# GpSimd takes over the epsilon add of the attention denominators

## The chip, the core and the metric

The kernel runs on one core of a Trainium2 chip. Its engines work at their own pace and wait for each other by semaphores: TensorE (PE: matmuls, with its weight loads as PEld), VectorE (DVE), ScalarE (ACT), GpSimd (POOL) and SyncE (SP), which here issues the DMAs. The metric is the device time of one execution in microseconds (us), the median of several runs.

## The reference, cut to what matters

A batch of 8 sequences of 512 positions and 128 features passes through 8 layers of linear attention with a feed-forward part, and beside them through a small routed expert network that gates the result. The part that the change touches is the normaliser of the attention:

```python
q = _phi((h @ wq + bq_).reshape(b, s, H, DH))      # H = 16 heads, DH = 8, _phi = elu + 1
k = _phi((h @ wk + bk_).reshape(b, s, H, DH))
kv = jnp.einsum('bshd,bshm->bhdm', k, v)
z = 1.0 / (jnp.einsum('bshd,bhd->bsh', q, k.sum(axis=1)) + 1e-06)
att = jnp.einsum('bshd,bhdm,bsh->bshm', q, kv, z).reshape(b, s, d)
h = _ln(h + att @ wo + bo_, g1_, be1_)
y = gelu(h @ w1 + c1_) @ w2 + c2_
h = _ln(h + y, g2_, be2_)
```

## The kernel before

A unit `u` is one sequence in one layer: `u = 8 * l + b` for layer `l` and sequence `b`, 64 units in all. Every engine runs an order written out by hand, a software pipeline of periods. In period `p`, PE does the key, value and output products of unit `p` (`pe_kz`, `pe_kv_ksum`, `pe_kvo`, `pe_att`), the feed-forward products of unit `p - 2` (`pe_up`, `pe_down`) and the key and query projections of unit `p + 1` (`pe_kq`).

DVE in period `p` makes the denominators of unit `p`: `dve_q_ks` multiplies q by the key sums, `dve_den` sums over each head into `den` (128x64), `dve_blocks` masks the key-value product, `dve_rden` adds the epsilon into `den_e` and takes the reciprocal `rden`, and `dve_q_n` scales q by it. Between the last two stand the small shift operations (`m_r` and `shift`) and the four normalisations of `dve_norm1` for unit `p - 1`, whose result PE transposes, ACT copies (`z1_hi`) and DVE splits (`dve_z1_lo`). `dve_k_floor` for unit `p + 1` follows `dve_kvo`; it counts the semaphore `tk`. In the trace, `z1_tm` and `z_tm` are both shown as `z_tm`, `z1_lo` as `z_lo`, and `w2_use` as `w_use`.

GpSimd computes the residuals in the form that the adds of DVE need. In its period `p` it makes `res_att` of unit `p` (line 1008 multiplies, line 1011 adds, both 128x512), which `dve_h1` reads in DVE's period `p + 1`, and then `res_ffn` of unit `p - 2` (lines 1019 and 1022), which `dve_h2` reads in DVE's period `p`. `pool_res_ffn` waits for `tk` to reach `u + 3`, which is the end of `dve_k_floor` of unit `p`, in DVE's period `p - 1`. So GpSimd is ahead of DVE: it makes `res_att` of unit `p` at the start of DVE's period `p - 1`, once `h1` of unit `p - 2` is done, and `res_ffn` of unit `p - 2` late in that same period.

Beside the residuals, GpSimd copies the weights of a new layer into place. With `b == 0` it copies `w_v` after `res_att` and `w_o` after `res_ffn` (`pool_wo`); with `b == 2` it renews `g_ffn` and `ffn_row` ahead of `res_ffn` and copies `w2_use` behind it (`pool_w2`, 128x512). PE waits for these copies in the period of the same number: `w_o` in front of `pe_kvo` with `b == 0`, and `w2_use` in front of the first two tiles of `pe_down` with `b == 2`. This holds for layers 1 to 7; layer 0 has its weights early.

Of the kernel before, what the change touches and what calls it, by code (L numbers as in the profile page):

```python
# [8 lines left out]
DEN_EPS = 1e-6  # L9


def build(nc, x, Wq, bq, Wk, bk, Wv, bv, Wo, bo, g1, be1, g2, be2, W1, c1, W2, c2, gf, bef,
# [4 lines left out]
    ALU = mybir.AluOpType  # L17
# [18 lines left out]
    with ExitStack() as ctx:  # L36
        def sb(name, shape, dt=F32):
            return ctx.enter_context(nc.sbuf_tensor(name, shape, dt))
# [4 lines left out]
        def sem(name):  # L43
            return ctx.enter_context(nc.semaphore(name))
# [65 lines left out]
        den = sb("den", [P, HT])  # L110
        den_e = sb("den_e", [P, HT])
# [42 lines left out]
        s = {n: sem(n) for n in names}  # L154
# [117 lines left out]
        def pool_qk(pool, l):  # L272
            pool.wait_ge(s["fold_a"], l)
            pool.wait_ge(s["kqproj"], l * SEQS)
            pool.sem_inc(s["pool_waited"], 1)
            nc.gpsimd.tensor_copy(w_kq_hi[:, :], fold_att[:, 0:2 * D]).then_inc(s["qk_ready"], 1)
            pool.wait_ge(s["qk_ready"], l * 2 + 1)
            nc.gpsimd.tensor_tensor(w_kq_lo[:, :], fold_att[:, 0:2 * D], w_kq_hi[:, :].bitcast(F32),
                                    ALU.subtract).then_inc(s["qk_ready"], 1)

        def pool_wv(pool, l):
            pool.wait_ge(s["kv_ps_s"], l * SEQS)
            pool.sem_inc(s["pool_waited"], 1)
            nc.gpsimd.tensor_copy(w_v[:, :], fold_att[:, 2 * D:3 * D]).then_inc(s["wv_ready"], 1)

        def pool_wo(pool, l):
            pool.wait_ge(s["kvo_ps_s"], l * SEQS)
            pool.sem_inc(s["pool_waited"], 1)
            nc.gpsimd.tensor_copy(w_o[:, :], raw_wo[:, :]).then_inc(s["wo_ready"], 1)

        def pool_att_rows(pool, l):

            pool.wait_ge(s["t2m"], l * SEQS)
            pool.sem_inc(s["pool_waited"], 1)
            nc.gpsimd.tensor_copy(g_att[:, :], raw_g[:, 0, :]).then_inc(s["gatt_ready"], 1)
            nc.gpsimd.tensor_tensor(att_row[:, :], row_sum[:, 0, :], raw_g[:, 0, :], ALU.subtract).then_inc(s["gatt_ready"], 1)
# [331 lines left out]
        def is_unit(u):  # L628
            return not isinstance(u, int) or 0 <= u < UNITS
# [4 lines left out]
        def after_first(u):  # L634
            return not isinstance(u, int) or u > 0

        def is_layer(l):
            return not isinstance(l, int) or l < L
# [365 lines left out]
        def pool_res_att(pool, u, b):  # L1004
            z_ready(pool, u)
            if after_first(u) and after_first(u - 1):
                pool.wait_ge(s["h1_s"], u - 1)
            nc.gpsimd.tensor_tensor(res_att[:, b % 2, :, :], z_tm[:, b, :, :], g_att[:, :].unsqueeze(1).to_broadcast([P, TT, D]),  # L1008
                                    ALU.mult).then_inc(s["t2a"], 1)
            pool.wait_ge(s["t2a"], u + 1)  # L1010
            nc.gpsimd.tensor_tensor(res_att[:, b % 2, :, :], res_att[:, b % 2, :, :], att_row[:, :].unsqueeze(1).to_broadcast([P, TT, D]),  # L1011
                                    ALU.add).then_inc(s["t2m"], 1)
# [12 lines left out]
        def pool_period(pool, l, b):  # L1025
            p = l * SEQS + b
            in_use = not isinstance(l, int) or l > 0
            if b == 0 and is_unit(p):
                if in_use:
                    pool_att_rows(pool, l)  # L1030
                pool.wait_ge(s["gatt_ready"], l * 2 + 2)
            if is_unit(p):
                pool_res_att(pool, p, b)
            if b == 0 and is_unit(p) and in_use:
                pool_wv(pool, l)
            if b == SEQS - 1 and is_layer(l + 1):
                pool_qk(pool, l + 1)
            if b == 2 and is_unit(p):
                if in_use:
                    pool_ffn_rows(pool, l, True)  # L1040
                pool.wait_ge(s["gffn_ready"], l * 2 + 2)
            if is_unit(p - 2):
                pool_res_ffn(pool, p - 2, (b - 2) % SEQS)
            if b == 0 and is_unit(p) and in_use:
                pool_wo(pool, l)
            if b == 2 and is_unit(p) and in_use:
                pool_w2(pool, l, True)
            if b == 5 and is_layer(l + 1):
                pool_rows(pool, l + 1)
# [25 lines left out]
        def dve_den(dve, u):  # L1075
            dve.wait_ge(s["q_ks_s"], u + 1)
            if after_first(u):
                dve.wait_ge(s["den_e_s"], u)
            nc.vector.tensor_reduce(den[:, :], q_ks[:, :, :].rearrange("p t (h d) -> p (t h) d", d=DH), AX.X,
                                    ALU.add).then_inc(s["den_s"], 1)  # L1080

        def dve_rden(dve, u):
            dve.wait_ge(s["den_s"], u + 1)
            if after_first(u):
                dve.wait_ge(s["rden_s"], u)
            nc.vector.tensor_scalar(den_e[:, :], den[:, :], DEN_EPS, None, ALU.add).then_inc(s["den_e_s"], 1)
            dve.wait_ge(s["den_e_s"], u + 1)
            if after_first(u):
                dve.wait_ge(s["qn"], u)
            nc.vector.reciprocal(rden[:, :], den_e[:, :]).then_inc(s["rden_s"], 1)  # L1090
# [146 lines left out]
        with nc.Block() as block:  # L1237
# [54 lines left out]
            @block.gpsimd  # L1292
            def _(pool):
                c = s["const_ready"]
                nc.gpsimd.memset(ident[:, :], 0.0).then_inc(c, 1)
                nc.gpsimd.memset(mean_f32[:, :], 1.0 / D).then_inc(c, 1)
                nc.gpsimd.memset(eps_col[:, :], EPS).then_inc(c, 1)
                nc.gpsimd.memset(ones[:, :], 1.0).then_inc(c, 1)
                pool.wait_ge(c, 4)
                nc.gpsimd.affine_select(out=ident[:, :], in_=ident[:, :], pattern=[[-1, P]], compare_op=ALU.not_equal,  # L1300
                                        fill=1.0, base=0, channel_multiplier=1).then_inc(c, 1)
                pool.wait_ge(c, 5)
                nc.gpsimd.tensor_tensor(centre[:, :], ident[:, :], mean_f32[:, :], ALU.subtract).then_inc(c, 1)
                pool.wait_ge(c, CONSTS_EARLY)
                nc.gpsimd.affine_select(out=head_mask[:, :], in_=ones[:, :], pattern=[[-DH, D // DH], [0, DH]],
                                        compare_op=ALU.is_ge, fill=0.0, base=0, channel_multiplier=1).then_inc(c, 1)
                pool.wait_ge(c, 7)
                nc.gpsimd.affine_select(out=head_mask[:, :], in_=head_mask[:, :], pattern=[[DH, D // DH], [0, DH]],
                                        compare_op=ALU.is_ge, fill=0.0, base=DH - 1, channel_multiplier=-1).then_inc(c, 1)
                nc.gpsimd.memset(raw_g[:, 0, :], 1.0).then_inc(c, 1)  # L1310
                nc.gpsimd.memset(raw_rows[:, R_BE2P, :], 0.0).then_inc(c, 1)
                pool.wait_ge(c, 10)
                pool_rows(pool, 0)
                pool_att_rows(pool, 0)
                pool.wait_ge(s["raw_wo0"], 16)
                pool.sem_inc(s["pool_waited"], 1)
                nc.gpsimd.tensor_copy(w_o[:, :], raw_wo[:, :]).then_inc(s["wo_ready"], 1)
                pool_period(pool, 0, 0)
                pool_ffn_rows(pool, 0, False)
                pool.wait_ge(s["raw_w20"], 16)  # L1320
                pool_w2(pool, 0, False)
                pool_period(pool, 0, 1)
                pool.wait_ge(s["t2m"], 2)
                nc.gpsimd.memset(e_hid[HID:HID + 1, :, :], 1.0).then_inc(c, 1)
                pool.wait_ge(c, 11)
                nc.gpsimd.iota(expert_m8[:, :], pattern=[[1, E]], base=-E, channel_multiplier=0,
                               allow_small_or_imprecise_dtypes=True).then_inc(c, 1)
                pool.wait_ge(c, CONSTS)
                for b in range(2, SEQS):
                    pool_period(pool, 0, b)  # L1330
                for l in range(1, L - 1):
                    for b in range(SEQS):
                        pool_period(pool, l, b)
                for b in range(SEQS):
                    pool_period(pool, L - 1, b)
                pool_period(pool, L, 0)
                pool_period(pool, L, 1)
                for i in (2, 4):
                    final_gate(nc.gpsimd, pool, i)
                    final_residual(nc.gpsimd, pool, EXPERTS[i])  # L1340
                    if i == 2:
                        final_residual(nc.gpsimd, pool, EXPERTS[1])
# [205 lines left out]
```

## Time and profile before

| What | Value |
|---|---|
| median of 3 runs | 873.08 us (872.48 to 874.48) |
| the profiled execution | 874.67 us |
| its span | 873.0 us |
| mean granted clock of TensorE, as a share of full speed | 0.972 |
| PE busy | 818.8 us (94%) |
| DVE busy | 795.7 us (91%) |
| ACT busy | 720.0 us (82%) |
| POOL busy | 376.9 us (43%) |

The span is what the profile covers; the profiled execution took 1.7 us more than that. A share of busy time is a mean over stages, so it doesn't say by itself which engine the others wait for.

### The profile page before, as it was taken

Reading aid. Unit: us, or ns where it says so; the run is one execution under the profiler, and the core shown is the slowest. Engines: PE = TensorE matmul, PEld = TensorE weight load, DVE = VectorE, ACT = ScalarE, POOL = GpSimd, SP = SyncE. Lnnn points to the kernel's source line nnn. Section 1 sums busy time; section 2 is a strip of 40 time slices with the busy share of each in tenths; the row PEclk is TensorE's granted clock in tenths of the full one; section 3 lists DMA queues with packets and bytes.
Section 4 is the critical chain, followed back from the end, with each engine's and each line's share of the span. In section 5 each row is a group of like instructions: output and inputs, shape, how many; then the busy total and the mean of one; then the engine's idle time right before and its main releaser. Section 6 shows DMA issues by size and latency. Waiting matters only on the chain.

```text
span 873.0 us, 19269 instructions
## 1 busy us (share of the span) xinstructions
PE 818.8 (94%) x5914; PEld 742.1 (85%) x5914; DVE 795.7 (91%) x2763; ACT 720.0 (82%) x1271; POOL 376.9 (43%) x362
## 2 busy tenths in 40 slices
PE   5698999999999999999999999999999999977776
PEld 4588899999999999999998999999999999876653
DVE  6888999989899999989899999989999989999998
ACT  2579999989998899989998899889998999654543
POOL 5234445445454444445445445354443544332113
PEclk9899999999999999999999999999999999999995
DMA  5300201010010101020010101010010000000002
GB/s 146 88 2 2 43 2 24 12 29 16 2 34 2 43 2 35 1 44 2 2 34 2 44 1 35 1 44 2 1 35 1 1 2 1 20 7 1 1 1 97
DMA packets 26264, 18.76 MB, mean 21 GB/s; under 512 B 4354, under 2 KB 22195, under 8 KB 26164
## 3 DMA queue, kind: packets, MB, share of 16 engines
q1 hardware_dynamic: 25300, 16.95, 7.4%
q8 instruction: 49, 0.80, 0.4%
q10 hardware_dynamic: 864, 0.59, 0.2%
q14 instruction: 51, 0.42, 0.2%
HBM read 15.43 MB, written 2.10 MB: 20 GB/s over the span
## 4 chain that ended last, share of the span: by engine, by line
PE 77%; DVE 14%; ACT 5%; issue 4%; DMA 0%; ACTq 0%; DVEq 0%
PE down_ps L749 20%; PE small_ps L682 6%; PE att_ps L712 6%; PE up_ps L741 5%; PE up_ps L739 5%; PE up_ps L740 5%; PE t_ps L660 4%; PE t_ps L719 3%; PE kq_ps L672 3%; PE kq_ps L673 3%; PE kq_ps L674 3%; DVE z_lo L1001 2%; ACT z_hi L900 2%; PE up_ps L703 2%; PE small_ps L690 2%
## 5 line engine op out<-in xcount | busy, mean ns | idle before, releaser
L749 PE MATMUL down_ps<-w_use,hid 128*128 128x128 f32 x2048 | 261.3, 276 | 0.7 <-ACT hid L851 0.7
L749 PEld LDWEIGHTS down_ps<-w_use,hid 128*128 128x128 f32 x2048 | 245.8, 193 | 1.9 <-ACT hid L851 1.1
L1019 POOL TENSOR_TENSOR res_ffn<-z_tm,g_ffn 128x512 f32<-128x512 f32 x64 | 82.7, 1292 | 265.4 <-DVE k_e L1103 240.9
L1008 POOL TENSOR_TENSOR res_att<-z_tm,g_att 128x512 f32<-128x512 f32 x64 | 82.5, 1288 | 174.3 <-DVE h L961 174.3
L851 ACT ACTIVATE hid<-up_ps 128x512 f32<-128x512 f32 x192 | 113.7, 592 | 30.7 <-PE up_ps L741 23.2
L973 DVE BATCH_NORM_STATS2 st<-h 128x6 f32<-128x128 f32 x512 | 109.1, 275 | 0.1
L906 ACT ACTIVATE z_tm<-h,shift,rstd 128x128 f32<-128x128 f32 x224 | 91.7, 482 | 0.0
L739 PE MATMUL up_ps<-z_hi,w_hi 128*128 128x512 f32 x192 | 86.2, 449 | 0.7 <-DVE z_lo L1001 0.7
L1022 POOL TENSOR_TENSOR res_ffn<-res_ffn,ffn_row 128x512 f32<-128x512 f32 x64 | 84.2, 1315 | 5.0
L1011 POOL TENSOR_TENSOR res_att<-res_att,att_row 128x512 f32<-128x512 f32 x64 | 82.4, 1287 | 5.0
L672 PE MATMUL kq_ps<-w_kq_hi,zq_hi 128*128 128x256 f32 x256 | 83.0, 324 | 1.5 <-DVE zq_lo L921 1.5
L946 ACT ACT_TABLE_LOAD x63 | 80.8, 1283 | 1.1
L930 ACT ACT_TABLE_LOAD x62 | 79.5, 1283 | 1.1
L741 PE MATMUL up_ps<-z_lo,w_hi 128*128 128x512 f32 x192 | 75.9, 396 | 0.0
L740 PE MATMUL up_ps<-z_hi,w_lo 128*128 128x512 f32 x192 | 75.4, 393 | 0.0
L682 PEld LDWEIGHTS small_ps<-k_phi,z_tm 128*128 128x128 f32 x512 | 68.1, 194 | 7.8 <-DVE k_phi L1110 2.3
L673 PE MATMUL kq_ps<-w_kq_lo,zq_hi 128*128 128x256 f32 x256 | 73.9, 289 | 0.0
L996 DVE TENSOR_SCALAR z_tm<-h,rstd,shift 128x128 f32<-128x128 f32 x256 | 71.5, 343 | 2.6 <-DVE shift L988 0.3
L674 PE MATMUL kq_ps<-w_kq_hi,zq_lo 128*128 128x256 f32 x256 | 73.8, 288 | 0.0
L1001 DVE TENSOR_TENSOR z_lo<-t_ps,z_hi 128x512 fp32r<-128x512 f32 x64 | 44.3, 692 | 32.1 <-ACT z_hi L900 32.1
L682 PE MATMUL small_ps<-k_phi,z_tm 128*128 128x128 f32 x512 | 68.7, 278 | 2.1 <-DVE k_phi L1110 2.1
L712 PE MATMUL att_ps<-kvo,q_n 128*128 128x128 f32 x512 | 69.3, 280 | 0.2 <-ACT q_n L893 0.2
(191 smaller groups left out, 1964.8 us busy)
## 6 DMA issues: line engine op xcount, KB each, us to landing
raw_w<-in_L_attn_W SPq DMA_DIRECT2D x15, 256.0 KB, 4.6
out_y<-gate_tm SPq DMA_DIRECT2D x8, 256.0 KB, 2.2
bias_bc<-in_L_attn_c SPq DMA_DIRECT2D x7, 256.0 KB, 4.5
x_tm<-in_L_attn_x SPq DMA_DIRECT2D x3, 512.0 KB, 7.8
raw_rows<-in_L_attn_be SPq DMA_DIRECT2D x15, 64.0 KB, 4.1
raw_g<-in_L_attn_g SPq DMA_DIRECT2D x14, 64.0 KB, 3.2
x_tm<-in_L_attn_x SPq DMA_DIRECT2D x2, 256.0 KB, 3.3
raw_rows<-in_L_attn_bo SPq DMA_DIRECT2D x8, 64.0 KB, 4.1
```

Of the source, the lines that this page charges most:

```text
L672: nc.tensor.matmul(to, tile(zq_hi, t), w_kq_hi[:, :], start=True, stop=False)
L673: nc.tensor.matmul(to, tile(zq_hi, t), w_kq_lo[:, :], start=False, stop=False)
L674: last = nc.tensor.matmul(to, tile(zq_lo, t), w_kq_hi[:, :], start=False, stop=True)
L682: last = nc.tensor.matmul(G_PS, z_tm[:, b, t, :], k_phi[:, t, :], start=(t == 0), stop=(t == TT - 1))
L712: last = nc.tensor.matmul(att_ps[:, t, :], tile(q_n, t), kvo[:, :], start=True, stop=True)
L739: nc.tensor.matmul(up_bank[j], w_hi, z1_hi[:, :], start=True, stop=False)
L740: nc.tensor.matmul(up_bank[j], w_lo, z1_hi[:, :], start=False, stop=False)
L741: nc.tensor.matmul(up_bank[j], w_hi, z1_lo[:, :], start=False, stop=True).then_inc(s["up"], 1)
L749: last = nc.tensor.matmul(down_ps[:, t, :], hid[:, j, t * P:(t + 1) * P], w2_use[:, j, :], start=(j == 0), stop=(j == FC - 1))
L851: nc.scalar.activation(hid[:, j, :], up_bank[j], ACT.Gelu).then_inc(s["gelu"], 1)
L906: nc.scalar.activation(z_tm[:, b, t, :], h2[:, b % 2, t, :], ACT.Identity, scale=rstd[:, i:i + 1], bias=shift[:, i:i + 1]).then_inc(s["z2n ...
L973: nc.vector.bn_stats(st[:, first + t, :], h[:, t, :]).then_inc(s[st_s], 1)
```

## The change

The add of the epsilon leaves `dve_rden` and becomes `pool_den` on GpSimd, between `res_att` of unit `p` and `res_ffn` of unit `p - 2`. GpSimd there waits for `den` of unit `p`, and DVE's reciprocal waits for GpSimd's `den_e`.

```diff
@@ pool_period
                 pool_wv(pool, l)
             if b == SEQS - 1 and is_layer(l + 1):
                 pool_qk(pool, l + 1)
+            if is_unit(p):
+                pool_den(pool, p)
             if b == 2 and is_unit(p):
                 if in_use:
                     pool_ffn_rows(pool, l, True)
@@
+        def pool_den(pool, u):
+            pool.wait_ge(s["den_s"], u + 1)
+            if after_first(u):
+                pool.wait_ge(s["rden_s"], u)
+            nc.gpsimd.tensor_scalar(den_e[:, :], den[:, :], DEN_EPS, None, ALU.add).then_inc(s["den_e_s"], 1)
+
         def dve_rden(dve, u):
-            dve.wait_ge(s["den_s"], u + 1)
-            if after_first(u):
-                dve.wait_ge(s["rden_s"], u)
-            nc.vector.tensor_scalar(den_e[:, :], den[:, :], DEN_EPS, None, ALU.add).then_inc(s["den_e_s"], 1)
             dve.wait_ge(s["den_e_s"], u + 1)
             if after_first(u):
                 dve.wait_ge(s["qn"], u)
@@ the constants of GpSimd's start
                 pool.wait_ge(s["t2m"], 2)
+                pool.wait_ge(s["den_e_s"], 2)
                 nc.gpsimd.memset(e_hid[HID:HID + 1, :, :], 1.0).then_inc(c, 1)
```

GpSimd's queue at a layer's third sequence (`b == 2`, layer 1), before, with the semaphores that each instruction waits for:

```order
L1008 TENSOR_TENSOR res_att<-z_tm,g_att 128x512 [waits h1_s,z2n]
L1011 TENSOR_TENSOR res_att<-res_att,att_row 128x512 [waits t2a]
L302 COPY g_ffn<-raw_g 128x128 [waits t1m]
L303 TENSOR_TENSOR ffn_row<-row_sum,raw_g 128x128
L1019 TENSOR_TENSOR res_ffn<-z1_tm,g_ffn 128x512 [waits z1n,tk,h2_s,gffn_ready]
L1022 TENSOR_TENSOR res_ffn<-res_ffn,ffn_row 128x512 [waits t1a]
L309 COPY w2_use<-raw_w2 128x512 [waits down]
```

And with the change:

```order
L1008 TENSOR_TENSOR res_att<-z_tm,g_att 128x512 [waits h1_s,z2n]
L1011 TENSOR_TENSOR res_att<-res_att,att_row 128x512 [waits t2a]
L1089 TENSOR_SCALAR den_e<-den 128x64 [waits rden_s,den_s]
L302 COPY g_ffn<-raw_g 128x128 [waits t1m]
L303 TENSOR_TENSOR ffn_row<-row_sum,raw_g 128x128
L1019 TENSOR_TENSOR res_ffn<-z_tm,g_ffn 128x512 [waits z1n,tk,h2_s,gffn_ready]
L1022 TENSOR_TENSOR res_ffn<-res_ffn,ffn_row 128x512 [waits t1a]
L309 COPY w_use<-raw_w 128x512 [waits down]
```

Everything from `g_ffn` to `w2_use` now stands behind a wait for `den` of unit `p`; before, nothing in this queue waited for it.

DVE's queue around the denominators of a unit, before:

```order
L1079 TENSOR_REDUCE den<-q_ks 128x64
L1059 TENSOR_TENSOR blk<-small_ps,head_mask 128x128
L1086 TENSOR_SCALAR den_e<-den 128x64
L1090 RECIPROCAL rden<-den_e 128x64
L984 TENSOR_TENSOR m_r<-mv,rstd 128x8
L988 TENSOR_SCALAR shift<-m_r 128x8
L996 TENSOR_SCALAR z_tm<-h,rstd,shift 128x128 x4
L1097 SCALAR_TENSOR_TENSOR q_nt<-q_elu,rden 128x512
```

And with the change:

```order
L1081 TENSOR_REDUCE den<-q_ks 128x64
L1061 TENSOR_TENSOR blk<-small_ps,head_mask 128x128
L1095 RECIPROCAL rden<-den_e 128x64
L984 TENSOR_TENSOR m_r<-mv,rstd 128x8
L988 TENSOR_SCALAR shift<-m_r 128x8
L996 TENSOR_SCALAR z_tm<-h,rstd,shift 128x128 x4
L1102 SCALAR_TENSOR_TENSOR q_nt<-q_elu,rden 128x512
```

One instruction is gone from DVE's queue, and the reciprocal behind it waits for GpSimd.

## Rows read from the trace of the kernel before

**Rows 1.** Stretch: us, busy (count) of PE, PEld, DVE, ACT, POOL; clock; DMA, GB/s

```profile
400.00:500.00 100.00, 99.67 (x754) 92.28 (x752) 92.47 (x316) 91.35 (x162) 47.77 (x47) 1.00 0.07 18
```

**Rows 2.** The chain that ended last, one period: start, us, what

```profile
442.83 1.78 PE down_ps L749 x16
...
447.61 0.63 PE t_ps L660 x4
...
454.66 1.78 PE down_ps L749 x16
```

**Rows 3.** Who waited for whom: us in total, times, longest

```profile
POOL res_ffn L1019 <- DVE k_e L1103: 240.9, 62, 6.6
...
DVE z_lo L1001 <- ACT z_hi L900: 32.1, 63, 1.8
```

**Rows 4.** Timeline of DVE in one period (layer 4, b = 2): start, us

```profile
442.48 0.65 DVE L1079 TENSOR_REDUCE den<-q_ks 128x64 f32<-128x512 f32 x1
...
443.25 0.18 DVE L1086 TENSOR_SCALAR den_e<-den 128x64 f32<-128x64 f32 x1
443.47 0.55 DVE L1090 RECIPROCAL rden<-den_e 128x64 f32<-128x64 f32 x1
443.94 0.10 DVE L984 TENSOR_TENSOR m_r<-mv,rstd 128x8 f32<-128x8 f32 x1
444.08 0.17 DVE L988 TENSOR_SCALAR shift<-m_r 128x8 f32<-128x8 f32 x1
444.29 1.12 DVE L996 TENSOR_SCALAR z_tm<-h,rstd,shift 128x128 f32<-128x128 f32 x4
445.32 0.68 DVE L1097 SCALAR_TENSOR_TENSOR q_nt<-q_elu,rden 128x512 f32<-128x512 f32 x1
...
446.12 0.42 DVE L1103 TENSOR_SCALAR k_e<-k_e 128x512 f32<-128x512 f32 x1
446.84 0.69 DVE L1001 TENSOR_TENSOR z_lo<-t_ps,z_hi 128x512 fp32r<-128x512 f32 x1 [0.30 <-ACT z_hi L900]
```

**Rows 5.** Timeline of POOL in that period: start, us

```profile
446.71 1.28 POOL L1019 TENSOR_TENSOR res_ffn<-z_tm,g_ffn 128x512 f32<-128x512 f32 x1 [3.47 <-DVE k_e L1103]
```

**Rows 6.** DVE and POOL, timelines at one place (layer 2, b = 1)

```profile
241.77 1.14 DVE L224 TENSOR_TENSOR w_lo<-fold_w,w_hi 128x512 fp32r<-128x512 f32 x1
...
241.09 1.27 POOL L1019 TENSOR_TENSOR res_ffn<-z_tm,g_ffn 128x512 f32<-128x512 f32 x1 [3.92 <-DVE k_e L1103]
242.44 1.62 POOL L1022 TENSOR_TENSOR res_ffn<-res_ffn,ffn_row 128x512 f32<-128x512 f32 x1
```

**Rows 7.** All instances of one line: shortest, median, longest ns

```profile
L1103 DVE TENSOR_SCALAR k_e<-k_e x64: 412/418/1061, 15.2 to 799.7; 128x512 f32<-128x512 f32 x64
L996 DVE TENSOR_SCALAR z_tm<-h,rstd,shift x256: 336/342/349, 37.3 to 829.9; 128x128 f32<-128x128 f32 x128
```

**Rows 8.** DVE and POOL in the tail, timelines

```profile
830.15 1.13 DVE L1131 SCALAR_TENSOR_TENSOR last_t<-h,mv,fin_bc 128x128 f32<-128x128 f32 x4
831.32 3.11 DVE L1135 SCALAR_TENSOR_TENSOR z_tm<-last_t,rstd,fin_bc 128x128 f32<-128x128 f32 x4
...
830.37 2.04 POOL L1019 TENSOR_TENSOR res_ffn<-z_tm,g_ffn 128x512 f32<-128x512 f32 x1 [11.45 <-issue]
```

**Rows 9.** Groups by line: count, busy us, mean ns of one

```profile
L1086 DVE TENSOR_SCALAR den_e<-den 128x64 f32<-128x64 f32 x64 | 13.1, 205 | 0.0
...
L309 POOL COPY w_use<-raw_w 128x512 f32<-128x512 f32 x8 | 4.9, 608 | 0.0
L303 POOL TENSOR_TENSOR ffn_row<-row_sum,raw_g 128x128 f32<-128x128 f32 x8 | 3.7, 460 | 0.0
L302 POOL COPY g_ffn<-raw_g 128x128 f32<-128x128 f32 x8 | 2.5, 315 | 0.0
```

**Rows 10.** Busy us and granted clock in two stretches of layer 7, columns as above

```profile
789.50:792.90 3.40, 1.09 (x5) 0.56 (x3) 3.37 (x12) 2.48 (x3) 0.00 (x0) 1.00 0.00 0
792.90:796.30 3.40, 3.03 (x14) 3.04 (x15) 3.40 (x24) 0.00 (x0) 2.54 (x2) 0.50 0.02 5
```

## The prediction

> **What bounds the kernel now.** I began with the busy times by stretch. In the middle of the run PE is busy for 99.67 us of 100 at its full clock, DVE for 92.47, POOL for 47.77 [rows 1]. So PE is the bound there, and whatever is taken off DVE is taken off an engine that isn't. The chain that ended last says the same: one period runs from 442.83 to 454.66, 11.83 us, all of it on PE [rows 2]. Then the waits: GpSimd waits for DVE's `k_floor` before nearly each `res_ffn`, 240.9 us in 62 waits, and DVE for ACT's `z_hi` before `z_lo`, 32.1 us in 63, a mean of 0.51 us [rows 3]. The second is the only slack that DVE has between its denominators and PE's next need of it. Last I read one period of both engines closely. From the end of `den` at 443.13 (442.48 + 0.65) DVE runs on to the end of `k_floor` at 446.54 (446.12 + 0.42) with no GpSimd instruction beside it; `res_ffn` begins at 446.71 [rows 4, 5]. The reader is to see that quiet stretch, since the change ends it.
>
> **What moves.** The add on DVE took 0.205 us in the mean, 13.1 us over 64 units [rows 9]. On GpSimd it is a wait in an in-order queue. Behind it stand `res_ffn` (two operations of 1.27 us), and then `res_att` of the next unit (two more), whose own conditions (`h1` and the state of earlier units) are long met by then. So four operations of about 1.27 us follow the add back to back, right where DVE used to be alone. In place of their present homes, `res_ffn` starts some 3.2 us earlier within a period but one period nearer to its reader, and `res_att` about 3 us after `res_ffn`. Neither is late for DVE's `h1` and `h2`: `h2` comes after `z_lo` and `k_phi`, over 4 us after `den`, and `res_ffn` is done 3.1 us after it.
>
> **The round trip.** DVE to GpSimd takes 0.17 us (446.54 to 446.71) [rows 4, 5]. GpSimd's add of 128x64 isn't in the trace; DVE's takes 0.18, GpSimd's copy of twice the size 0.315 and its two-input add of that size 0.460 [rows 4, 9]. I take 0.28, nearest to the copy since it has one input, so `den_e` is ready at 443.58 and the reciprocal starts at about 443.62 in place of 443.47: 0.15 us later (0.05 to 0.4 by the bounds). `blk` on DVE covers the rest. This alone hides in the 0.51 us of slack.
>
> **The collision.** While a GpSimd two-input operation runs, some DVE operations don't. `w_lo`, issued at 241.77 under `res_ffn`, took 1.14 where `z_lo`, of the same form but with an input in PSUM, took 0.69 in the same surroundings: it began its work at about 242.22, which is 0.14 before GpSimd's end at 242.36. GpSimd's next operation, at 242.44, then took 1.62 instead of 1.28 [rows 4, 5, 6]. It goes one at a time. `k_floor`, with one SBUF input and a constant, is of that kind too: 418 ns, but 1061 the one time that GpSimd ran beside it. `norm1` has never been tried: 256 instances between 336 and 349 [rows 7]. It is the same operation as `k_floor` and I take it as blocked; `q_nt` has two inputs in SBUF, like `w_lo` and like the `L1135` group of the tail, whose four took 3.11 against 1.13 for the four before [rows 8]. DVE operations that read PSUM (`z_lo`) ran beside GpSimd untouched at 0.69.
>
> Now one period, in the times of [rows 4]. GpSimd's four operations are A, B, C, D. A runs from 443.55 to 444.82. `m_r` would start at 444.09, gets through at 444.68 and ends at about 444.79 instead of 444.04: +0.75, the round trip included. B starts 0.08 after A's end, at 444.90, and holds until 446.03. It blocks `shift` or the first `norm1`, which starts at 446.03 for 444.29: +1.74. For C there are two ways. In the tail GpSimd, issued at 830.37 into a row of DVE operations, took 2.04 and didn't get in before the row ended: DVE in a close row keeps its turn [rows 8]. Then `norm1` and `q_nt` pass, C runs from 447.7, and `k_floor`, due at 447.86, waits until 448.83: +0.97, 2.7 in all, and D falls behind it and costs nothing. Or C gets between two `norm1` (+1.1), as happened to the `L1135` group, of which more than one was held (3.11 - 1.13 = 1.98, against 1.13 for one blockage) [rows 8]; then D blocks `k_floor` (+0.97): 3.8 in all. From either, 0.51 us of slack at `z_lo` comes off: 2.2 or 3.3 us per period.
>
> The Trainium skill ("SBUF — State Buffer", Who interferes with whom) describes this as an exclusive lock on a port pair: whichever engine issues first has it for its whole instruction, and the other is fully blocked: "Issue order, not op shape, decides who blocks". By that rule C, issued ahead of the second `norm1`, would always get in. The row at 830.37 speaks against that, the one at 831.32 for it.
>
> **Where it lands.** PE's transposes at 447.61 wait for `z_lo`, and from there to 454.66 PE has 7.05 us of its own work up to the next `down`, which leads to the next `den` [rows 2]. Nothing in that part gets shorter, so the delay is added once in every period: 62 of them, as many as GpSimd's waits [rows 3]. At 2.2 us that is 136 us, at 3.3 it is 205. DVE and GpSimd miss each other by hundredths of a us at these points, so I expect both ways, from period to period: 2.75 x 62 = 170 us.
>
> **The copies behind the wait.** With `b == 2` of layers 1 to 7, `w2_use` comes after the add, `g_ffn` 0.315, `ffn_row` 0.460, `res_ffn` 2.62 and its own 0.608, which is 4.0 us after 443.58, so 447.6 [rows 5, 6, 9]. PE wants it at 442.83: it stands for 4.7 us. It then needs 4.78 (447.61 - 442.83) to its transposes, at 452.4, where the collision alone puts them at 449.8 or 450.9 [rows 2]. That is 1.5 to 2.6 more, 7 times: 15 us. `w_o` (`b == 0`) is ready at 443.58 + 2.62 + 0.3 = 446.5 where PE wants it at 444.61; with the 1.1 us of PE work behind it the `z1` transposes start at 447.6, 0.5 after `norm1`, which hides under the blocked `k_floor`: nothing. The copies of `w_v` and `w_kq`, ahead of the add, end about 7 us after a `den`, and PE reads them nearly 10 after it: nothing. The seven `w_lo` lose their 0.45 of collision: -3.
>
> **The clock.** In layer 7, a stretch of 3.4 us with PE busy for 1.09 was followed by one at half the clock, 1.2 for 2.4 GHz [rows 10]. The waits for `w2_use` are longer than that, and I add 7 x 1.5 = 10 us. In the second way of C, PE idles some 2.5 us in one piece per period (`norm1` ends at 448.3 or later, PE is there at 445.73); a halved stretch then costs up to 1.7 us. If half of the periods lost 1 us, that would be 31 more. In the first way the piece is 1.4 us, and I expect nothing.
>
> **Sum.** Against the profiled execution, 874.7: + 170 + 15 + 10 - 3 = 1067. That execution is 0.2% over the median of 873.08, which is also about what a measurement here can tell from no change.
>
> **Rivals.**
> 1. C always gets in: 874.7 + 205 + 12 + 10 - 3 = 1099, and up to 1130 with the clock. Chance 0.20. This is what the Trainium skill's section named above would have.
> 2. DVE's rows always hold: 874.7 + 136 + 18 + 10 - 3 = 1036, down to 1010 if `shift` and `norm1` pass more easily. Chance 0.14.
> 3. `norm1` and `q_nt` aren't blocked, or GpSimd yields. Then only the copies cost. For `w2_use` 4.7, for `w_o` 446.5 - 444.6 = 1.9, 7 times each: 46 us, so 921. For it: `norm1` was never seen beside GpSimd. Against it: `k_floor` at 1061. Chance 0.08.
> 4. Faster: the freed time of DVE pays, at most the whole 13.1 us, so 861. It needs `w2_use` to be ready when PE comes to it, 442.83, which is 0.3 us before `den` itself has ended, and PE to be no bound. PE at 99.67 speaks against it. Chance 0.02. No change at all: 0.02.
> 5. Slower than 1130: the half clock in most periods, or a `den_e` on GpSimd of 0.6 us and more, which would move everything. Chance 0.07.
>
> The mixed case has 0.45, with its own range of 1045 to 1090; 0.02 is left for times between 930 and 1005. From 1005 to 1130 stand 0.45 + 0.20 + 0.14 = 0.79. Slower by over 0.2% has 0.96.
>
> **What would show it.** The period grows from 11.83 to 14 or 15 us in all layers, and to 16 or 17 with `b == 2`. The mean of `norm1` rises over 0.45 us, that of `k_floor` over 1, while `z_lo`, `k_phi` and `h2` stay at 0.68. GpSimd waits for `den`, no longer for `k_floor`; PE waits for `norm1` and `z_lo` in every period and for `w2_use` seven times. PE's busy share falls to about 77%. If `norm1` stays at 342 ns, the collision is the wrong step, and 921 is the number.

## The result and the profile after

The changed kernel takes 1149.25 us (median of 4 runs, 1148.05 to 1152.44), the kernel before 873.78 us beside it (4 runs, 872.48 to 875.23): a ratio of 1.316, 95% interval 1.312 to 1.319. The forecast was 1067 us, 1005 to 1130. The direction was right and so was the place of the collision; the time lies above the range.

The page of the profile after, parts 1 and 2 (busy us by engine, then tenths of TensorE's granted clock in 40 slices):

```profile
span 1148.3 us, 19270 instructions
...
PE 910.4 (79%) x5914; PEld 830.9 (72%) x5914; DVE 997.6 (87%) x2699; ACT 725.2 (63%) x1271; POOL 403.5 (35%) x426
...
PEclk9889898899889898999988998998989898888896
```

PE's share is 79% where it was 94%, and DVE has gained 202 busy us although it has 64 instructions fewer. The clock is below full speed all along the run; before, it stood at 1.00 in the middle stretch [rows 1]. Where DVE's time went, by its lines (all instances: shortest, median, longest ns):

```profile
L996 DVE TENSOR_SCALAR z_tm<-h,rstd,shift x256: 333/1179/1429, 38.3 to 1105.2; 128x128 f32<-128x128 f32 x128
...
L988 DVE TENSOR_SCALAR shift<-m_r x64: 169/171/173, 38.1 to 1104.1; 128x8 f32<-128x8 f32 x56, 128x4 f32<-128x4 f32 x8
...
L1102 DVE SCALAR_TENSOR_TENSOR q_nt<-q_elu,rden x64: 676/679/1664, 25.8 to 1091.2; 128x512 f32<-128x512 f32 x64
...
L1108 DVE TENSOR_SCALAR k_e<-k_e x64: 407/413/1297, 15.6 to 1074.1; 128x512 f32<-128x512 f32 x64
...
L1115 DVE SCALAR_TENSOR_TENSOR k_phi<-kq_ps,k_e x64: 673/680/692, 16.6 to 1075.9; 128x512 f32<-128x512 f32 x64
```

`norm1` (L996), 336 to 349 ns in all its 256 instances before [rows 7], now has a median of 1179. `shift` is never touched, `q_nt` once, and `k_phi`, which reads PSUM, not at all. `k_floor` (L1108) is held in 21 of 64, with a mean of 641 ns. `m_r` is held in 63 of 64. One period shows how (layer 4 of 0 to 7, timelines of POOL and DVE; start, us; the four `norm1` are shown from three overlapping windows):

```profile
567.61 0.37 POOL L1089 TENSOR_SCALAR den_e<-den 128x64 f32<-128x64 f32 x1 [10.52 <-DVE den L1081]
568.06 1.27 POOL L1019 TENSOR_TENSOR res_ffn<-z_tm,g_ffn 128x512 f32<-128x512 f32 x1
569.41 1.28 POOL L1022 TENSOR_TENSOR res_ffn<-res_ffn,ffn_row 128x512 f32<-128x512 f32 x1
570.65 1.26 POOL L1008 TENSOR_TENSOR res_att<-z_tm,g_att 128x512 f32<-128x512 f32 x1
571.99 1.26 POOL L1011 TENSOR_TENSOR res_att<-res_att,att_row 128x512 f32<-128x512 f32 x1
...
568.54 0.82 DVE L984 TENSOR_TENSOR m_r<-mv,rstd 128x8 f32<-128x8 f32 x1
569.39 0.17 DVE L988 TENSOR_SCALAR shift<-m_r 128x8 f32<-128x8 f32 x1
...
569.60 1.18 DVE L996 TENSOR_SCALAR z_tm<-h,rstd,shift 128x128 f32<-128x128 f32 x1
...
570.70 2.64 DVE L996 TENSOR_SCALAR z_tm<-h,rstd,shift 128x128 f32<-128x128 f32 x2
...
571.92 1.67 DVE L996 TENSOR_SCALAR z_tm<-h,rstd,shift 128x128 f32<-128x128 f32 x2
...
575.43 0.69 DVE L1001 TENSOR_TENSOR z_lo<-t_ps,z_hi 128x512 fp32r<-128x512 f32 x1 [0.70 <-ACT z_hi L900]
```

GpSimd's operations A, B, C, D each meet another of DVE's: A holds `m_r` (0.82 for 0.10), B the first `norm1` (1.18), C the second (570.70 to 572.00), D the third (571.92 to 573.34). The fourth ends at 573.59. The order of the records tells most of it: `shift` at 569.39 is 0.02 ahead of B and takes its usual 0.17, C at 570.65 is 0.05 ahead of the second `norm1` and holds it. It does not tell all: the third `norm1`, at 571.92, has its record 0.07 ahead of D's and is held all the same. In a row without gaps each of DVE's records begins some 0.08 before the one ahead of it ends (that one ends at 572.00, after D's start at 571.99), so the start of a record is not the start of its work.

This is the pattern with `b == 1`, 3, 4 and 6. With `b == 0` and 2 GpSimd's copies shift C and D to the third and fourth `norm1`. With `b == 5` and 7 C holds the fourth, D waits until `q_nt` is through (1.73 for 1.26) and then holds `k_floor` (layers 1 to 6).

What PE does meanwhile (timeline; then three stretches: us, busy and count of PE, PEld, DVE, ACT, POOL, and the granted clock):

```profile
573.65 1.12 PE L719 MATMUL t_ps<-ident,z_tm 128*128 128x128 f32 x4 [3.39 <-DVE z_tm L996]
574.56 1.06 PE L703 MATMUL up_ps<-ident,q_nt 128*128 128x128 f32 x4
575.41 1.83 PE L749 MATMUL down_ps<-w_use,hid 128*128 128x128 f32 x8
577.08 0.60 PE L660 MATMUL t_ps<-ident,z_tm 128*128 128x128 f32 x4
```

```profile
569.60:573.60 4.00, 0.66 (x6) 0.46 (x5) 4.00 (x5) 1.16 (x3) 3.57 (x3) 1.00 0.00 0
573.60:577.00 3.40, 3.35 (x16) 3.35 (x17) 2.70 (x6) 1.93 (x3) 0.00 (x0) 0.50 0.00 0
577.00:580.40 3.40, 3.40 (x27) 3.23 (x27) 3.40 (x9) 3.17 (x7) 0.00 (x0) 1.00 0.00 0
```

PE stands for 3.39 us in front of the transposes of `z1` and then works at 1.2 GHz for 3.4 us: these transposes take 1.12 where they took 0.60 before, eight `down` matmuls 1.83 for 1.06. The waits in total:

```profile
POOL den_e L1089 <- DVE den L1081: 675.1, 64, 14.9
ACT z_hi L900 <- PE t_ps L719: 262.6, 64, 8.1
PEld t_ps L719 <- DVE z_tm L996: 101.0, 32, 4.8
...
PE down_ps L749 <- POOL w_use L309: 32.8, 7, 4.7
...
PE small_ps L695 <- POOL w_o L289: 12.8, 7, 1.8
```

GpSimd now waits for `den` and no longer for `k_floor` [rows 3]. The waits for `w2_use` and `w_o` are there 7 times each, 4.7 and 1.8 us long, where 4.7 and 1.9 were worked out.

From the timelines of all units in layers 1 to 6 I took two lengths of the period (means): from the end of `den` to the start of `z_lo`, and from there to the end of the next `den`. They were 4.06 and 8.05 us before (12.11 in all) and are 8.00 and 8.74 after (16.74). The experiments are read by the same two.

### The profile page after: what moved, and what is told of

It is laid out like the page before. It is cut to its first block, busy times and chain, and to the rows that moved or that the text cites. A ratio compares the mean times of both kernels' runs of the same rounds, so it can differ in the third digit from the quotient of the medians.

```text
span 1148.3 us, 19270 instructions
## 1 busy us (share of the span) xinstructions
PE 910.4 (79%) x5914; PEld 830.9 (72%) x5914; DVE 997.6 (87%) x2699; ACT 725.2 (63%) x1271; POOL 403.5 (35%) x426
## 4 chain that ended last, share of the span: by engine, by line
issue 63%; POOL 30%; DVE 4%; PE 1%; POOLq 0%; ACT 0%; DMA 0%; ACTq 0%; DVEq 0%
POOL res_ffn L1019 7%; POOL res_att L1008 7%; POOL res_att L1011 7%; POOL res_ffn L1022 5%; POOL den_e L1089 2%; POOL w_kq_lo L278 1%; DVE st L973 1%; DVE fin_t L1148 0%; DVE last_t L1136 0%; DVE z_tm L1140 0%; DVE gate_tm L1169 0%; DVE z_tm L1152 0%; POOL w_use L309 0%; DMA raw_att<-in_L_attn_Wv 0%; POOL att_row L296 0%
## 5 line engine op out<-in xcount | busy, mean ns | idle before, releaser
L749 PE MATMUL down_ps<-w_use,hid 128*128 128x128 f32 x2048 | 308.5, 308 | 33.4 <-POOL w_use L309 32.8
L749 PEld LDWEIGHTS down_ps<-w_use,hid 128*128 128x128 f32 x2048 | 291.2, 223 | 36.1 <-POOL w_use L309 34.2
L1089 POOL TENSOR_SCALAR den_e<-den 128x64 f32<-128x64 f32 x64 | 23.6, 368 | 675.1 <-DVE den L1081 675.1
L996 DVE TENSOR_SCALAR z_tm<-h,rstd,shift 128x128 f32<-128x128 f32 x256 | 239.5, 995 | 11.1 <-POOL res_ffn L1019 8.8
L900 ACT ACTIVATE z_hi<-t_ps 128x512 fp32r<-128x512 f32 x64 | 38.2, 597 | 262.6 <-PE t_ps L719 262.6
L719 PE MATMUL t_ps<-ident,z_tm 128*128 128x128 f32 x256 | 50.8, 332 | 155.3 <-DVE z_tm L996 94.7
L719 PEld LDWEIGHTS t_ps<-ident,z_tm 128*128 128x128 f32 x256 | 33.3, 165 | 165.6 <-DVE z_tm L996 101.0
L1074 DVE SCALAR_TENSOR_TENSOR q_ks<-q_elu,small_ps 128x512 f32<-128x512 f32 x64 | 43.9, 686 | 46.1 <-PE small_ps L691 46.1
L712 PE MATMUL att_ps<-kvo,q_n 128*128 128x128 f32 x512 | 82.6, 315 | 0.0
L712 PEld LDWEIGHTS att_ps<-kvo,q_n 128*128 128x128 f32 x512 | 79.6, 237 | 0.2 <-ACT q_n L893 0.2
```

What stands on the lines that cost most here:

```text
L712: last = nc.tensor.matmul(att_ps[:, t, :], tile(q_n, t), kvo[:, :], start=True, stop=True)
L719: last = nc.tensor.transpose(t_ps[:, t * P:(t + 1) * P], z1_tm[:, t, :], ident[:, :])
L749: last = nc.tensor.matmul(down_ps[:, t, :], hid[:, j, t * P:(t + 1) * P], w2_use[:, j, :], start=(j == 0), stop=(j == FC - 1))
L996: nc.vector.tensor_scalar(z1_tm[:, t, :], h1[:, t, :], rstd[:, t:t + 1], shift[:, t:t + 1], ALU.mult, ALU.add).then_inc(s["z1n"], 1)
```

## The experiments

Short diffs are against the changed kernel unless it says otherwise. `DEN` stands for `if is_unit(p): pool_den(pool, p)` in `pool_period`.

**1. The add for the unit before.**

```diff
             if is_unit(p):
                 pool_res_att(pool, p, b)
+            if is_unit(p - 1):
+                pool_den(pool, p - 1)
...
-            if is_unit(p):
-                pool_den(pool, p)
```

(Beside this, the wait for `den_e_s` at GpSimd's start is lowered from 2 to 1.)

> The add stays on GpSimd, but of the unit before: right behind res_att of unit p it adds for unit p - 1, which is the unit whose den DVE makes at that time, and res_ffn follows only after k_floor, as before. If the wait's place is the cause (my theory), nothing runs beside m_r and norm1, norm1 is back at 342 ns, the reciprocal starts 0.13 to 0.16 us later than before, that hides in the 0.5 us that z_lo waits, and the time is 870 to 878. If the round trip of the add itself counts, it adds up to 0.3 us in each of 62 periods: 885 to 893. If GpSimd's add as such is the cause, it stays near 1149.

Measured: 879.39 us beside 873.16, ratio 1.007 (1.005 to 1.009). The collision is gone, with `norm1` at 342 ns in the mean (groups by line: count, busy us, mean ns), while DVE still waits for GpSimd's add 64 times (waits: total, times, longest):

```profile
L996 DVE TENSOR_SCALAR z_tm<-h,rstd,shift 128x128 f32<-128x128 f32 x256 | 71.4, 342 | 2.5 <-DVE shift L988 0.2
```

```profile
DVE rden L1095 <- POOL den_e L1089: 21.3, 64, 0.4
```

So of 275 us, 6 belong to the add on GpSimd and its round trip, and some 269 to where it stands. The 6 are outside what I had written (870 to 878), though: the part up to `z_lo` is 0.10 us longer, 4.16, and that was to be hidden.

**2. The wait alone**, against the kernel before, whose DVE goes on adding:

```diff
             if b == SEQS - 1 and is_layer(l + 1):
                 pool_qk(pool, l + 1)
+            if is_unit(p):
+                pool.wait_ge(s["den_s"], p + 1)
```

> The kernel before with one line more: GpSimd waits for den of unit p between its two residuals, and DVE adds the epsilon itself as before. By my theory all of the loss is in this wait: the period is 16 to 16.7 us in place of 12.1, norm1 near 1 us in the mean, 1120 to 1150. If the add or its round trip is a large part, the time falls well below, and with a harmless wait it is 874.

Measured: 1129.03 us, ratio 1.293 (1.290 to 1.296). `norm1`:

```profile
L996 DVE TENSOR_SCALAR z_tm<-h,rstd,shift 128x128 f32<-128x128 f32 x256 | 240.2, 997 | 11.2 <-POOL res_ffn L1019 8.8 <-DVE shift L988 0.3
```

One line of waiting, without any work moved, makes 256 of the 275 us. Without the add in front of it A begins 0.46 us sooner after `den` and `m_r` 0.16 (medians, `b == 3`), and the part up to `z_lo` is 0.36 shorter (7.64).

**3. The copies ahead of the wait.**

```diff
+            if b == 2 and is_unit(p):
+                if in_use:
+                    pool_ffn_rows(pool, l, True)
+                pool.wait_ge(s["gffn_ready"], l * 2 + 2)
+            if b == 0 and is_unit(p) and in_use:
+                pool_wo(pool, l)
+            if b == 2 and is_unit(p) and in_use:
+                pool_w2(pool, l, True)
             DEN
```

(and the same lines removed behind `DEN` and behind `res_ffn`).

> The changed kernel with the copies of g_ffn, ffn_row, w2_use and w_o moved ahead of the wait for den. The wait of PE for w2_use (32.8 us in 7) and for w_o (12.8 us in 7) disappears. In the changed kernel a period with b = 2 takes 19.3 us against 16.8 of its neighbours, so I expect 7 x 2.5 = 18 us less, near 1131. If PE's waits counted in full beside the collision it would be 46 us, near 1103; if they were all hidden, 1149.

Measured: 1142.10 us, ratio 1.308 (1.304 to 1.311), 7 us less than the changed kernel and not 18. The periods with `b == 2` did come down, from 19.3 to 16.9 us (medians). That is 17 us in 7 periods; some 10 came back in the others, most with `b == 6` (18.1 for 17.0). The part from `z_lo` to `den`, where nothing was touched, has 9.12 us for 8.74 in the mean, and with `b == 2` 9.44 for 7.98. PE's work is the same there, so this pointed at the clock.

**4. Unread matmuls in PE's stop**, 24 of them:

```diff
+                if att:
+                    pe.wait_ge(s["zq_lo_s"], p + 2 if state else UNITS)
+                    for _ in range(24):
+                        nc.tensor.matmul(t_ps[:, 0:P], ident[:, :], ident[:, :], start=True, stop=True)
                 pe_z1_transpose(pe, p - 1, p + 2 if state else UNITS)
```

> The changed kernel, with 24 matmuls of 128x128 by 128 that nobody reads in front of PE's transposes of z1, where PE stands for some 3.3 us in each period; they take about 2.7 us and work on a PSUM bank that the transposes overwrite. It adds work and takes none away. If the halved clock after that stop costs about 1 us per period (the part from z_lo to the next den is 8.74 us against 8.05 before, and the transposes take 0.8 for 0.5), the granted clock stays near 1.0 and the time falls by 40 to 60 us, to 1090 to 1110. If the clock costs nothing beside the collision, the time stays or grows.

Measured: 1257.76 us, ratio 1.440 (1.437 to 1.444). As a test of the time it failed by my sizing: each call shows as two matmuls, and the row is longer than the stop that it was to fill.

```profile
569.37 5.52 PE L835 MATMUL t_ps<-ident 128*128 128x128 f32 x48
```

But with a mean clock of 0.972, for 0.894 in the changed kernel, the part from `z_lo` to `den` was 7.98 us. So the clock explains the 0.7 us that this part had grown by.

**5. Half as many, 12**, otherwise as 4.

> As the kernel with 24 unread matmuls, but with 12 of them. The 24 took 5.5 us, 0.23 each and twice what I had assumed, longer than PE's stop of 3.4 to 3.9 us, so they pushed the transposes back; the 12 should take 2.8 us and fit. The part from z_lo to the next den was 7.98 us with the 24, at a clock of 0.97, and 8.74 in the changed kernel. If the halved clock costs what that says, and some 0.3 us more in the transposes of z1, the time is 1080 to 1100. If the clock's cost is only apparent (PE waits for DVE anyway), it stays at 1149.

Measured: 1120.81 us, ratio 1.284 (1.279 to 1.289): 28 us less than the changed kernel with more work in it, and less of a gain than I wrote. The periods of 5 of 8 sequences went down to between 15.4 and 15.5 us (from between 16.3 and 17.0), but with `b == 2` they grew to 21.0 from 19.3: PE has stood for `w2_use` there, has no stop left in front of the transposes, and does the 2.8 us of unread work on top.

**6. Copies ahead and 12 unread matmuls**, 3 and 5 together.

> The changed kernel with the copies ahead of the wait and the 12 unread matmuls. Moving the copies gave 7 us where 18 were expected, and its part from z_lo to den grew from 8.74 to 9.12. If the missing 10 us went to the clock (the periods fell so that more of them had the half clock in the part that counts), then against the kernel with the 12 matmuls alone moving the copies gives the full 17 to 20 us: 1063 to 1080. If the copies were worth only 7 us, it is 7 us below that kernel.

Measured: 1073.12 us, ratio 1.229 (1.227 to 1.232). Now each period of layers 1 to 6 takes 15.15 to 15.55 us (medians by sequence), and the clock stays at full speed (stretch of 100 us, columns as above):

```profile
400.00:500.00 100.00, 96.67 (x743) 89.91 (x742) 93.75 (x251) 72.96 (x130) 38.19 (x39) 1.00 0.06 18
```

Against 3 this is 69 us less, with the same wait for `den` and the same blocked `norm1`: the price of the clock once the copies are out of the way. With the copies behind the wait the same matmuls gave 28 (experiment 5), and with the matmuls in place moving the copies gave 48: the two terms are not independent, and 7 and 69 are one way of splitting 76. What is left, 1073.1 - 873.2 = 200 us, is the collision with the round trip in it.

**7. `res_att` held until `k_floor`.**

```diff
         def pool_res_att(pool, u, b):
             z_ready(pool, u)
+            pool.wait_ge(s["tk"], u + 1)
```

> The changed kernel, with res_att of the next unit held back until k_floor (one more wait on tk). Two of GpSimd's four operations leave the place of the collision, the wait for den and the copies stay as they are. If each operation costs DVE what it holds (1.1 us), norm1 is blocked once instead of three times: a mean of about 0.61 us for 0.995, and the period falls by 2.2 us and by the clock's part, to 13.5 us: 975 to 1000. If the loss were the wait's alone (copies, round trip), it stays near 1149.

Measured: 1005.10 us, ratio 1.152 (1.151 to 1.154). This is just outside the 975 to 1000 expected. One `norm1` of four is blocked in most periods, the group's mean is 558 ns where 610 was expected. Six of eight sequences have periods of 13.4 to 13.7 us; with `b == 0` and 2, where the copies still stand behind the wait, they are 15.3 and 19.2 (medians).

**8. Copies ahead, and the second operation of `res_ffn` held until `k_floor` of the period**, so that only A is left:

```diff
             pool.wait_ge(s["t1a"], u + 1)
+            pool.wait_ge(s["tk"], min(u + 4, UNITS))
```

> The changed kernel, with the copies ahead of the wait for den, and with the second operation of res_ffn (and so res_att behind it) held until k_floor of the same period. The wait for den stays where the change put it; only the first operation of res_ffn still runs beside DVE's m_r. By my theory norm1 is back at 342 ns, m_r stays at 0.8 us, of its 0.7 us 0.5 hide in the wait of z_lo, and the time is 880 to 905. If there is a cost of the wait beside collision, clock and copies, it shows here as more than that.

Measured: 929.11 us, ratio 1.064 (1.062 to 1.066), more than the 880 to 905 expected, for two reasons that the trace shows. `m_r` is late by A alone, `norm1` is at 348 ns in the mean, and yet `z_lo` starts 4.56 us after `den` where it started 3.72 (medians, `b == 3`): `norm1` ends 0.92 later, round trip included, and 0.84 of it arrives. And GpSimd's held operations meet the `zf` pair of `b == 2` and `b == 6`, whose periods are some 1 us longer than their neighbours'. That pair is a `tensor_scalar` of 128x128 like `norm1`, and 13 of its 32 were held in the kernel before already; here it is 26 (all instances of the line, before and here: shortest, median, longest ns):

```profile
L440 DVE TENSOR_SCALAR zf_tm<-x_tm,mv_x,r_f x32: 329/338/1424, 87.9 to 692.0; 128x128 f32<-128x128 f32 x32
...
L440 DVE TENSOR_SCALAR zf_tm<-x_tm,mv_x,r_f x32: 323/620/1439, 90.6 to 733.2; 128x128 f32<-128x128 f32 x32
```

**9. `norm1` in another form**, with the shift as its second SBUF input:

```diff
-                nc.vector.tensor_scalar(z1_tm[:, t, :], h1[:, t, :], rstd[:, t:t + 1], shift[:, t:t + 1],
-                                        ALU.mult, ALU.add).then_inc(s["z1n"], 1)
+                nc.vector.scalar_tensor_tensor(z1_tm[:, t, :], h1[:, t, :], rstd[:, t:t + 1],
+                                               shift[:, t:t + 1].to_broadcast([P, D]),
+                                               ALU.mult, ALU.add).then_inc(s["z1n"], 1)
```

> The changed kernel with norm1 written as scalar_tensor_tensor, the shift being its second SBUF input: the same result, and an operation of the form that in the tail of the kernel before ran four in a row while GpSimd was held off. If rows of that form keep their turn where rows of tensor_scalar don't, norm1 is blocked once and not three times, and 2.2 us per period come back: 1000 to 1020. If GpSimd gets between any two DVE operations of either form, the time stays at 1140 to 1155.

Measured: 1160.60 us, ratio 1.330 (1.327 to 1.332), a little above even the second range of 1140 to 1155. The form is no protection:

```profile
L996 DVE SCALAR_TENSOR_TENSOR z_tm<-h,rstd,shift x256: 336/1246/1421, 37.6 to 1114.0; 128x128 f32<-128x128 f32 x128
```

The tail of this run says more. The row of four `last_t` at 830.15 [rows 8], which kept GpSimd waiting, stands in all twelve kernels here. In eleven of them it holds GpSimd for 0.77 us, as in the changed kernel (POOL, then DVE):

```profile
1105.72 2.04 POOL L1019 TENSOR_TENSOR res_ffn<-z_tm,g_ffn 128x512 f32<-128x512 f32 x1 [11.37 <-issue]
...
1105.50 1.14 DVE L1136 SCALAR_TENSOR_TENSOR last_t<-h,mv,fin_bc 128x128 f32<-128x128 f32 x4
```

Here, with the `last_t` lines unchanged, GpSimd gets in behind the first, and the second and third are held:

```profile
1114.43 1.27 POOL L1020 TENSOR_TENSOR res_ffn<-z_tm,g_ffn 128x512 f32<-128x512 f32 x1 [11.38 <-issue]
...
1114.22 3.24 DVE L1137 SCALAR_TENSOR_TENSOR last_t<-h,mv,fin_bc 128x128 f32<-128x128 f32 x4
```

GpSimd's record begins 0.043 to 0.048 us ahead of the second `last_t` in the eleven, and 0.050 ahead here.

**10. GpSimd sent into the running row**, against the kernel before:

```diff
         def pool_res_att(pool, u, b):
             z_ready(pool, u)
+            if u >= 2:
+                pool.wait_ge(s["z1n"], TT * (u - 2) + 1)
```

> The kernel before, with res_att of the next unit held until the first of the four norm1 of a period has ended, so that GpSimd asks for its first operation while the row of norm1 is already running, not ahead of it. GpSimd does nothing else that is new. If a running row keeps its turn (as in the tail at 830.37), all four norm1 stay at 0.34 us, res_att gets in behind q_nt and blocks k_floor once, to 1.3 to 1.4 us; k_floor is not in front of z_hi, so about 0.5 us per period is lost: 895 to 920. If GpSimd gets in at the next border between two norm1, one or two of them take 1.2 to 1.4 us, all of it reaches z_hi, and the time is 960 to 1020.

Measured: 988.35 us, ratio 1.132 (1.130 to 1.134). GpSimd gets in (POOL, then DVE from two windows):

```profile
501.64 1.27 POOL L1010 TENSOR_TENSOR res_att<-z_tm,g_att 128x512 f32<-128x512 f32 x1 [7.62 <-DVE z_tm L996]
502.99 1.26 POOL L1013 TENSOR_TENSOR res_att<-res_att,att_row 128x512 f32<-128x512 f32 x1
...
501.43 0.34 DVE L996 TENSOR_SCALAR z_tm<-h,rstd,shift 128x128 f32<-128x128 f32 x1
...
501.68 2.66 DVE L996 TENSOR_SCALAR z_tm<-h,rstd,shift 128x128 f32<-128x128 f32 x2
```

GpSimd's operation begins while the second `norm1` runs, 0.04 us ahead of the third; the third is held until it is over, and the fourth by the next one. This row, at least, does not keep its turn.

## Why the prediction was wrong, point by point

The differences add up as follows, with the terms of the prediction beside them. The clock's is the difference of experiments 3 and 6, the copies' of the changed kernel and experiment 3, and the rest is experiment 6 against the kernel before. Taken in the other order (experiments 5 and 6), the clock has 28 and the copies 48; the 200 and the sum of the two, 76 for the predicted 25, stay.

| Term | Predicted, us | Measured, us |
|---|---|---|
| collision, with the round trip | 170 - 3 | 200 |
| copies behind the wait | 15 | 7 |
| clock | 10 | 69 |
| sum | 192 | 276 |

**The clock is the step that failed most.** I priced the half clock for the seven waits for `w2_use` only, and left the other periods to a rival, since half of my periods were to have a stop of 1.4 us. The stop is 3.39 us in the period shown and has medians of 1.9 to 3.5 in six of the eight sequences, and in the middle of the run the granted clock is 0.88 to 0.91 in each 100 us. Experiments 3 and 6 show the price with the collision held equal: 69 us. What came was rival 5, "the half clock in most periods", which had a chance of 0.07. It also hid the term of the copies, of which 17 us went out of the periods with `b == 2` and some 10 came back as slower PE work in the others.

**The collision was right in kind and its size came from two misreadings.** The first: "I expect both ways, from period to period". In layers 1 to 6 C got in between `norm1` in every period, and the way in which it waits for `norm1` and `q_nt` never came. D got in too, except with `b == 5` and 7. Which way it goes did not change from period to period. Whether hundredths of a us can turn it is another question, which the tail leaves open. With one operation of GpSimd behind `den` (experiment 8), two (7) and four (the changed kernel), `z_lo` starts 4.56, 5.40 and 7.45 us after `den`, against 3.72 before (medians, `b == 3`): 0.84 for the first, 0.84 for the second, 2.05 for the last two together. The rival in which C always gets in had this right, but gave D the victim `k_floor`, which it had only with `b == 5` and 7; in the ordinary period that was the third `norm1`. Its 3.3 us per period meets the measured mean of 3.31 (below) by luck, since 0.51 was wrongly taken off it. A smaller slip: A was put at 443.55, before the add ahead of it is done at 443.58. It starts 0.08 after that end, and `m_r` ends 0.92 later for the 0.75 worked out.

The second: "From either, 0.51 us of slack at `z_lo` comes off". DVE did wait 0.51 us for ACT's `z_hi`, but `z_hi` descends from `norm1` by way of PE's transposes. A delay in front of `norm1` moves both sides of that wait, which was slack for `q_nt`, `kvo` and `k_floor` alone. What can hide is only the time by which `norm1` is done before PE comes to its transposes: in the kernel before 0.05 to 0.2 us with `b == 1`, 2, 3 and 6, and 0.3 to 0.6 with the others. So in experiment 8 0.84 of 0.92 arrive with `b == 3` but 0.11 of 0.46 with `b == 4`, and in the mean of layers 1 to 6 0.53 of 0.71. In experiment 1 it is 0.10 of 0.20, none of it with `b == 0`, 4, 5 and 7, which makes its 6 us.

Both errors make the estimate too small. They were partly made good by the 62 equal periods: layer 0 grew by only 2.0 us per period in experiment 6, and in layers 1 to 6 the mean was 3.31, below the 3.73 of the ordinary period, because with `b == 4`, 5 and 7 part of the delay hides in this way, and with `b == 5` and 7 D meets no `norm1`.

The Trainium skill ("SBUF — State Buffer", Who interferes with whom) says that issue order decides which of the two engines is fully blocked. In the periods of the changed kernel and in experiment 10 GpSimd, 0.04 to 0.07 us ahead by the records, blocked `norm1`, which agrees. I had held one row of the tail against it, `res_ffn` at 830.37 [rows 8], and weighed it as half of the evidence. The row stands in all twelve kernels, and in eleven of them GpSimd's record begins 0.043 to 0.048 us ahead and yet it is GpSimd that is held, for 0.77 us. In experiment 9 it is 0.050 ahead and gets in. A lead of 0.04 was enough against `norm1` in experiment 10. So the starts of the records do not always tell who issued first, and what decides in the tail stays open; it is not the form of the DVE operation alone, since the `last_t` lines are the same in all twelve. The mistake was to carry one row over to another place. The nearer row was the `zf` pair, of `norm1`'s own form and size, with 13 of 32 held in the kernel before; it would also have settled that `norm1` can be held.

**What held:** that the place of the wait and not the add is the cause (experiments 1 and 2), that `norm1` would be blocked though it had never been seen beside GpSimd, that `k_phi` and its like would not, that nothing in the eight us from `z_lo` to `den` makes good a delay, and the lengths of the two waits for weights. GpSimd's add takes 368 ns where I took 280, and the reciprocal starts 0.16 us later where 0.15 was worked out. **What did not hold** beside the sum: `k_floor` has a mean of 641 ns and not over 1000, since D's victim was mostly a `norm1`; and the periods are 15.2 to 17.0 us, 19.3 with `b == 2` (medians), for 14 to 15 and 16 to 17.

None of the versions beats the kernel before. With PE busy for 99.67 us of 100 [rows 1], there is nothing to win by unloading DVE in the middle of the run.

## What to carry to other kernels

A new wait in a queue should be priced by what stands behind it, and by what that work will now run beside; here a wait of one line, with no work moved, cost 29%. Before a wait in the profile is counted as slack, follow its releaser back: if it descends from the instruction that is being delayed, that wait hides nothing, and only what is spare on the way to it counts. And once a bounding PE starts to stop for 2 to 4 us in every period, its clock belongs in the sum; unread work in the stop measures that price, if it is sized to fit.

## What the runs showed of the hardware

- A GpSimd operation of 1.27 us on SBUF operands that got in first held off DVE's `norm1` (as `tensor_scalar` and with two SBUF inputs), `k_floor`, `q_nt` and even the 0.10 us of `m_r` (0.82), one for one: by 0.72 to 1.08 us in the period shown, and by less where the DVE operation came later in it (`m_r` 0.47 and 0.33 with `b == 4` and 5). `k_phi`, `z_lo` and DVE's reciprocal (0.55 us in all 64) kept their time.
- A row of DVE operations with no gap need not keep GpSimd out: in experiment 10 it entered behind the second of four. But the row of `last_t` in the tail kept it out for 0.77 us in eleven kernels of twelve, with leads of GpSimd's record that differ by less than 0.01 us from the twelfth's.
- A stretch of 4.0 us in which PE was busy for 0.66 was followed by 3.4 us at half the clock. 24 or 12 unread matmuls per period brought the mean clock from 0.89 to 0.97, and with the copies moved to 0.98; 12 of them made the kernel of experiment 3 6% faster (1142.1 to 1073.1 us), and the changed kernel 2.5% (1149.3 to 1120.8). The Trainium skill ("TensorE: Matmul & The Clock Gate", HAM oscillation — how this bites in real kernels) describes such stops between matmuls as lowering the clock again and again; the trace agrees.
